# Start of a compressed interaction network: the order of the first chunk's tiles, and how fields and first weights are loaded

## What is computed

```
z = relu(sum over h, k of x0[b,h,d] * xk[b,k,d] * W[h,k,s] + bias[s])      s = 0..127
```

## Time and profile before

| | |
|---|---|
| median of 3 runs | 562.16 us |
| the profiled execution, its own time | 562.33 us |
| its span, first to last instruction | 560.5 us |
| PE busy | 551.9 us, 98% |
| DVE busy | 535.9 us, 96% |
| GpSimd (POOL) busy | 499.5 us, 89% |
| ACT busy | 379.4 us, 68% |
| DMA | 122.17 MB, mean 218 GB/s |

### The profile page before, as it was taken

One profiled execution on the slowest core, in us unless ns is written; L12 is line 12 of the kernel. 1 busy time (PEld: TensorE's weight loads), 2 busy tenths in 40 slices (PEclk: granted clock), 3 DMA queues, 4 the chain that ended last, 5 costly groups with the idle time before them and its releaser, 6 DMA issues.

```text
span 560.5 us, 6190 instructions
## 1 busy us (share of the span) xinstructions
PE 551.9 (98%) x2008; PEld 374.9 (67%) x2008; DVE 535.9 (96%) x496; ACT 379.4 (68%) x427; POOL 499.5 (89%) x228
## 2 busy tenths in 40 slices
PE   7999999999999999999999999999999999999997
PEld 2435667667677677777767677677777767677665
DVE  4679999999999999999999999999999999999985
ACT  0436577776858767676776858777676876858662
POOL 0438899899999989999899999989999899999986
PEclk9999999999999999999999999999999999999999
DMA  8997391844828266391845828276391845826200
GB/s 326 418 408 317 132 370 34 325 191 181 344 87 331 108 254 271 146 361 30 331 183 183 342 95 333 98 262 263 150 363 29 333 177 192 333 99 215 81 1 20
DMA packets 21056, 122.17 MB, mean 218 GB/s; under 512 B 2720, under 2 KB 2976, under 8 KB 10784
## 3 DMA queue, kind: packets, MB, share of 16 engines
q1 hardware_dynamic: 20736, 121.51, 56.0%
q10 hardware_dynamic: 288, 0.26, 0.2%
HBM read 121.24 MB, written 0.52 MB: 217 GB/s over the span
## 4 chain that ended last, share of the span: by engine, by line
PE 82%; DVE 10%; issue 3%; ACT 2%; DMA 1%; POOL 1%; SPq 0%; DVEq 0%; POOLq 0%; ACTq 0%
PE z L611 82%; DVE raw L426 4%; DVE exact L426 3%; DVE d_raw L426 2%; DMA fields<-x_fields 1%; DVE lo L440 1%; POOL lo L515 1%; ACT hi L656 1%; ACT maps L675 0%; ACT final L696 0%; ACT L675 0%; DVE sums L453 0%; DVE sums L447 0%; SPq L358 0%; SPq L337 0%
## 5 line engine op out<-in xcount | busy, mean ns | idle before, releaser
L515 POOL TENSOR_TENSOR lo<-raw,hi 128x1024 fp32r<-128x1024 f32 x198 | 469.1, 2410 | 12.1 <-ACT hi L656 11.6
L656 ACT ACTIVATE hi<-raw 128x1024 fp32r<-128x1024 f32 (+1 forms) x213 | 219.1, 1029 | 125.1 <-DVE raw L426 112.0
L611 PE MATMUL z<-hi,w_hi 128*128 128x512 f32 (+1 forms) x559 | 220.8, 399 | 0.9 <-ACT hi L656 0.4
L426 DVE TENSOR_TENSOR raw<-spread,maps 128x1024 f32<-128x1024 f32 x184 | 219.0, 1210 | 2.1 <-ACT maps L675 2.1
L611 PE MATMUL z<-hi,w_lo 128*128 128x512 f32 x513 | 202.5, 395 | 0.0
L611 PE MATMUL z<-lo,w_hi 128*128 128x512 f32 x544 | 196.7, 451 | 0.2 <-POOL lo L515 0.2
L611 PE MATMUL z<-exact,w_exact 128*128 128x512 f32 (+1 forms) x386 | 180.4, 594 | 2.8 <-DVE exact L426 2.0
L611 PEld LDWEIGHTS z<-lo,w_hi 128*128 128x128 f32 x544 | 101.2, 188 | 56.2 <-issue 31.5
L611 PEld LDWEIGHTS z<-hi,w_hi 128*128 128x128 f32 (+1 forms) x559 | 104.8, 188 | 31.4 <-ACT final L696 3.7
L611 PEld LDWEIGHTS z<-exact,w_exact 128*128 128x128 f32 (+1 forms) x386 | 72.1, 189 | 68.0 <-issue 53.7
L611 PEld LDWEIGHTS z<-hi,w_lo 128*128 128x128 f32 x513 | 96.2, 188 | 22.9 <-issue 0.5
(11 more groups left out here) (21 smaller groups left out, 69.6 us busy)
## 6 DMA issues: line engine op xcount, KB each, us to landing
spread<-x_spread SPq DMA_DIRECT2D x80, 1024.0 KB, 8.1
fields<-x_fields SPq DMA_DIRECT2D x31, 768.0 KB, 6.8
fields<-x_fields SPq DMA_DIRECT2D x15, 512.0 KB, 5.6
w_exact<-w SPq DMA_DIRECT2D x10, 256.0 KB, 14.7
spread<-x_fields SPq DMA_DIRECT2D x1, 768.0 KB, 10.1
raw<-w SPq DMA_DIRECT2D x1, 640.0 KB, 6.7
spread<-x_fields SPq DMA_DIRECT2D x1, 512.0 KB, 10.7
out<-sums SPq DMA_DIRECT2D x2, 240.0 KB, 4.2
```

Of the source, the lines that this page charges most:

```text
L426: nc.vector.tensor_tensor(products, by_field, by[0:rows, :].unsqueeze(1).to_broadcast([rows, tiles, COLS]), ALU.mult).then_inc(ready, 1)
L515: nc.gpsimd.tensor_tensor(low_part(layer, c, k), raw[low_rows(layer, k), PLACE[S][layer, c, k] % RAW_RING, 0:tiles_in(layer, k), :], hi[lo ...
L611: mm = nc.tensor.matmul(z_of(layer, c)[:, :], w[0:rows, :], part[0:rows, :], start=(step == FIRST_STEP[layer, c] and p == 0), stop=(step = ...
L656: nc.scalar.activation(hi[0:rows, count % HI_RING, 0:tiles, :], products, ACT.Copy).then_inc(hi_ready, 1)
```

## The change

- Layer 0 of chunk 0 runs its couples in the order 3, 0, 1, 2 (`FIRST_ORDER`), on DVE and on PE. Later chunks keep 0, 1, 2, 3.
- The tiles of layer 0 are stored one place further on: tile 6 stands in place 0, tiles 0 to 5 in places 1 to 6 (`place0`), in the fields and in w0. The inputs are rolled on the host to match.
- The fields of each chunk come in four loads of two slots (512 KB each) in place of three. The early fields come as slot 0 (256 KB) and twice two slots (512 KB each), in place of 768 and 512 KB. Of chunk 1's own fields, slots 0 and 1 and slots 6 and 7 are loaded (512 KB each), in place of slot 0 and slots 5 to 7.
- w0 comes in three parts of one, two and four tiles (128, 256, 512 KB), all issued by ACT ahead of the bias; before, two and five tiles (256 KB from ACT, 640 KB from SP). DVE adds them in three instructions.
- In chunks other than 1 DVE waits for load 0 and for the couple's own load ahead of each of the four couples: eight waits on fields a chunk in place of three.
- `W2_EARLY` is 0, so the two places where it stands change nothing.

```diff
-W0_CUTS = (0, 2, TILES0)
-W0_PARTS = 2
+FIRST_ORDER = (3, 0, 1, 2)
+W0_CUTS = (0, 1, 3, TILES0)
+W0_PARTS = 3
+W2_EARLY = 0
-FIELD_CUTS = (0, 3, 5, 1 + TILES0)
+FIELD_CUTS = (0, 2, 4, 6, 1 + TILES0)
+FIELD_PARTS = 4
...
-    yield 0, 0, range(COUPLES[0])
+    yield 0, 0, FIRST_ORDER
...
+        def place0(t):
+            return (t + 1) % TILES0
...
-            load_fields(0, 0)
-            sp.dma_start(w0_staged[:, W0_CUTS[1]:, :, :], w0[:, W0_CUTS[1]:, :, :]).then_inc(w0_loaded[1], 16)
-            load_fields(0, 1)
-            load_fields(0, 2)
+            for p in range(FIELD_PARTS):
+                load_fields(0, p)
             load_early(0)
             load_early(1)
...
+                        first = place0(2 * k)
+                        part = (k + 1) % FIELD_PARTS
                         if ahead:
-                            dve.wait_ge(early_loaded[k], 16)
-                        elif k < 3:
-                            dve.wait_ge(fields_loaded[k], (c if c and k == 1 else c + 1) * 16)
+                            dve.wait_ge(early_loaded[k], 16 if k else 32)
+                            by, by_field = early[:, 0, :], early[:, first:first + tiles, :]
+                        else:
+                            if c != 1:
+                                dve.wait_ge(fields_loaded[0], (c + 1) * 16)
+                            dve.wait_ge(fields_loaded[part], (c if c and part in (1, 2) else c + 1) * 16)
+                            by = copies if c else field_copies
+                            by_field = fields[0:rows, 1 + first:1 + first + tiles, :]
...
             for p in range(W0_PARTS):
                 sum_weights0(p)
-                multiply(0, 0, range(p, p + 1))
-            multiply(0, 0, range(W0_PARTS, COUPLES[0]))
+                multiply(0, 0, FIRST_ORDER[p:p + 1])
+            multiply(0, 0, FIRST_ORDER[W0_PARTS:])
...
-                        if (layer, c) == (0, 0) and k < W0_PARTS:
-                            pe.wait_ge(w0_summed, k + 1)
+                        if (layer, c) == (0, 0):
+                            pe.wait_ge(w0_summed, min(FIRST_ORDER.index(k) + 1, W0_PARTS))
...
-            act.dma_start(w0_staged[:, 0:W0_CUTS[1], :, :], w0[:, 0:W0_CUTS[1], :, :]).then_inc(w0_loaded[0], 16)
+            for p in range(W0_PARTS):
+                a, e = W0_CUTS[p:p + 2]
+                act.dma_start(w0_staged[:, a:e, :, :], w0[:, a:e, :, :]).then_inc(w0_loaded[p], 16)
```

More of the change, by code:

```diff
@@ L262, in cin_kernel @@
         early_loaded = [sem(f"early_loaded{p}") for p in range(EARLY)]
-        fields_loaded = [sem(f"fields_loaded{p}") for p in range(3)]
+        fields_loaded = [sem(f"fields_loaded{p}") for p in range(FIELD_PARTS)]
         spread_loaded = [sem(f"spread_loaded{s}") for s in range(SPREAD_RING)]
@@ L332, in load_fields @@
                 if c == 1:
-                    if p == 1:
+                    if p in (1, 2):
                         return
-                    e = 1 if p == 0 else e
                 sp.dma_start(fields[:, a:e, :], x_fields[c, :, a:e, :]).then_inc(fields_loaded[p], 16)
             def load_early(p):
-                a, e = FIELD_CUTS[p:p + 2]
-                sp.dma_start(early[:, a:e, :], x_fields[1, :, a:e, :]).then_inc(early_loaded[p], 16)
+                if p == 0:
+                    sp.dma_start(early[:, 0, :], x_fields[1, :, 0, :]).then_inc(early_loaded[0], 16)
+                sp.dma_start(early[:, 1 + 2 * p:3 + 2 * p, :],
+                             x_fields[1, :, 2 + 2 * p:4 + 2 * p, :]).then_inc(early_loaded[p], 16)
             def load_spread(c, q):
@@ L366, in _ @@
             load_fields(1, 0)
-            load_fields(1, 2)
+            load_fields(1, 3)
             for p in range(QUADS):
@@ L374, in _ @@
                     wait_multiplied(sp, 0, c + 1, COUPLES[0] - 1)
-                    for p in range(3):
+                    for p in range(FIELD_PARTS):
                         load_fields(c + 2, p)
@@ L400, in multiply @@
                         ahead = c == 1 and k < EARLY
+                        first = place0(2 * k)
+                        part = (k + 1) % FIELD_PARTS
                         if ahead:
-                            dve.wait_ge(early_loaded[k], 16)
-                        elif k < 3:
-                            dve.wait_ge(fields_loaded[k], (c if c and k == 1 else c + 1) * 16)
-                        by = early[:, 0, :] if ahead else copies if c else field_copies
-                        by_field = (early if ahead else fields)[0:rows, 1 + 2 * k:1 + 2 * k + tiles, :]
+                            dve.wait_ge(early_loaded[k], 16 if k else 32)
[6 more added lines that the diff above has]
+                            by_field = fields[0:rows, 1 + first:1 + first + tiles, :]
                     else:
@@ L468, in weights0_last_split_lo @@
                 rows, last = slice(2 * BLOCK, ROWS_REST), len(SPLIT_TILES[0]) - 1
-                nc.vector.tensor_tensor(w_hi[0][rows, last, :], w_exact[0][rows, TILES0 - 1, :],
+                nc.vector.tensor_tensor(w_hi[0][rows, last, :], w_exact[0][rows, place0(TILES0 - 1), :],
                                         w_hi[0][rows, last, :].bitcast(fp32),
@@ L537, in weights0_split_lo @@
                 pool.wait_ge(weights_hi[0], 1)
-                nc.gpsimd.tensor_tensor(w_lo[0][:, 0:tiles, :], w_exact[0][:, 0:tiles, :],
+                nc.gpsimd.tensor_tensor(w_lo[0][:, 0:tiles, :], w_exact[0][:, 1:1 + tiles, :],
                                         w_hi[0][:, 0:tiles, :].bitcast(fp32),
@@ L599, in contract @@
                                 rows = HALF
-                            passes += [(w_exact[layer][:, t, :],
+                            passes += [(w_exact[layer][:, t if layer else place0(t), :],
                                         exact[:, count % EXACT_RING, t % 2, :], rows)]
@@ L620, in _ @@
                 nc.tensor.matmul(z[2][:, :], final[:, 0:OUT], final[:, :], start=True, stop=True)
-            contract(0, 0, range(COUPLES[0]))
+            contract(0, 0, FIRST_ORDER)
             contract(0, 1, range(EARLY))
@@ L644, in split_hi @@
                 for k in couples:
-                    if c == 0 and (layer == 1 or layer == 2 and k < KEPT):
+                    if c == 0 and (layer == 1 or layer == 2 and W2_EARLY <= k < KEPT):
                         weights_split_hi(layer, 2 * k)
@@ L708, in _ @@
                     tiles = len(SPLIT_TILES[0]) - 1
-                    nc.scalar.activation(w_hi[0][:, 0:tiles, :], w_exact[0][:, 0:tiles, :], ACT.Copy)
-                    nc.scalar.activation(w_hi[0][0:ROWS_REST, tiles, :], w_exact[0][0:ROWS_REST, TILES0 - 1, :],
+                    nc.scalar.activation(w_hi[0][:, 0:tiles, :], w_exact[0][:, 1:1 + tiles, :], ACT.Copy)
+                    nc.scalar.activation(w_hi[0][0:ROWS_REST, tiles, :], w_exact[0][0:ROWS_REST, place0(TILES0 - 1), :],
                                          ACT.Copy).then_inc(weights_hi[0], 1)
@@ L722, in _ @@
                     split_hi(0, c + 1, range(0, MAPS2_AT) if c else range(EARLY, COUPLES[0]))
+                if c == 0:
+                    for k in range(W2_EARLY):
+                        weights_split_hi(2, 2 * k)
                 spread_maps2(c)
@@ L750 @@
     x_fields[:, :, 1:][:, used] = x[:, right[used]]
+    x_fields[:, :, 1:] = np.roll(x_fields[:, :, 1:], 1, axis=2)
     pair = np.concatenate([x, x[:, -1:]], axis=1).reshape(CHUNKS, TILES, 2, COLS)
@@ L759 @@
     pairs[both, 1] = w0[right[both], i[both]]
-    arrays = {"x_fields": x_fields, "x_spread": x_spread, "w0": pairs}
+    arrays = {"x_fields": x_fields, "x_spread": x_spread, "w0": np.roll(pairs, 1, axis=1)}
     for n, w in ((1, L0_rec_w1), (2, L0_rec_w2)):
```

## The result

The changed kernel takes 563.33 us (median of 10 runs, 563.18 to 564.23) where the kernel before takes 562.20 (10 runs, 562.08 to 562.73) on the same chip: 1.1 us slower, ratio 1.0021 with a 95% interval of 1.0011 to 1.0031. Nine of the ten stand at 563.18 to 563.49 with a mean granted clock of 0.997, one at 564.23 with 0.994. The forecast was 562.2 in a range of 561.4 to 562.9, so the time lies outside it, on the slower side. The profiled execution took 563.21 us with a span of 561.4; before, 562.33 and 560.5.

What follows compares the result with a forecast made beforehand. PE and DVE were taken as both full from 50 to 540 us, so start delays reach the end. Gain 1.06 and loss 1.10 left 0.04 us: 562.33 + 0.04 = 562.37, median 0.17 under, so 562.2; range 561.4 to 562.9.

Steps and rivals of the forecast that it cites:

- The frame: Start: its price is when layer 0 of chunk 0 is contracted and ACT's table load starts, 15.43 before, 15.47 forecast.
- Step 1: End of layer 0, chunk 0, on PE: tile 6 no longer runs last, gain 1.06 us.
- How loads share the engines: First loads: queues alternate by packet; landing is 3.81 us + 2.46 ns per KB ahead; rounds at 5.38, 7.27, 9.79, 11.05.
- Steps 2 and 3: Start: couple 0 on PE at 8.89, costing nothing; couple 1 at 11.68, 1.25 us later, awaiting w0's third part.
- Rival D: Start: PE falls to its lower clock while waiting before couples 0 and 1, costing 3.4 us, 565.6; chance 0.03.
- B: Start: w0's third part lands ahead of fields 2, at 8.53, 0.6 us won, 561.6; chance 0.20.
- C: Later chunks: DVE's 70 extra waits are not hidden, 0.016 to 0.05 us each, 563.3 to 565.7; chance 0.05.
- The cap: Layer 1's start: first `spread` load lands at 17.4, layer 1 starts at 18.08, limiting any gain to 0.7 us.

Runs made afterwards that it cites:

- experiment 1: Changed kernel with two more zero matmuls on PE between the twelve-row tile and couple 0: 562.86 us, ratio to the kernel before 1.0007.
- experiment 4: Changed kernel with its new loads and layout, but couples in the old order 0, 1, 2, 3 in the first chunk: 564.35 us, ratio 1.0034.
- experiment 5: Changed kernel with two more zero matmuls before couple 0 and first-chunk queues exchanged (ACT issues fields, SP w0 and bias): 562.55 us, ratio 1.0002.
- experiments 4 and 6: The second of these: changed kernel with five zero matmuls at the start in place of three: 562.86 us, ratio 1.0005.
- experiment 7: Changed kernel with three loads of fields, w0 in two parts (second from SP), bias on SP, five zero matmuls: 561.73 us, ratio 0.9988.
- experiment 11: Changed kernel with two more zero matmuls before couple 0, w0's third part from SP, bias on SP behind the early fields: 562.20 us, ratio 0.9993.
- experiment 2: Changed kernel with w0's third part issued by SP between its loads 1 and 2 of the fields: 563.40 us, ratio 1.0018.
- experiment 8: Kernel before with five more met DVE waits ahead of each layer 0 couple in chunks 2 to 15, 280 in all: 562.75 us, ratio 1.0003.
- experiment 9: Kernel before with two zero matmuls at the start in place of three: 563.48 us, ratio 1.0016.

## Why the prediction was wrong

- **The frame held.** The time of the table load was the one number to work out. At 16.52 it is outside the 14.8 to 15.9 that I had allowed it. It moved by 1.09 us; the end moved by 0.88 in the profiled executions (563.21 against 562.33) and by 1.13 in the medians. In the profiled pair 13 chunks took 436.36 us after and 436.56 before, 0.2 less; experiment 1, which has all of the change's waits and later loads, took 436.56 like the kernel before, so that difference is not the change's; what it is stays open.
- **Step 1 (tile 6 leaves the end, 1.06 us) was right in size:** the order alone moved the table load by 0.92 (experiment 4 against the changed kernel, both with the clock down), and couple 1 had started some 0.15 earlier in experiment 4 (12.08 against 12.23).
- **"How loads share the engines" failed in its sums for rounds 2 and 3 (a round is load n of SP with load n of ACT), and this is the first step that went wrong.** Alternation by packet was right, and SP's fields landed at 7.3 and 9.8 as forecast. But I read the landings of a kernel in which ACT's queue had one load ahead of its bias, and took the two loads of a round to land together. ACT's came at 5.6, 7.77 and 10.33, behind the fields by 0.2, 0.5 and 0.5 us. Experiment 5 showed the queue to be the reason for which of the two is late. That the whole round ends near 10.3 whichever queue is late is not explained by it: in the profiles of experiments 4 and 6, with the same loads, the fields came at 10.0 and 9.9, and w0's third part still at 10.3. The number of loads does not explain it either. The changed kernel issues three loads more ahead of `spread`, and the third of these lands at 24.09 instead of 23.68, 0.14 us a load; but experiment 7, with one load more than the kernel before, has it at 23.59, earlier and not later. Experiment 11 rules the bias out. Why the round is late stays open.
- **Steps 2 and 3 carried it on:** couple 0 on PE at 9.40, not 8.89, couple 1 at 12.23, not 11.68. With the clock up this is 0.49 us over the forecast (15.96 against 15.47, experiment 1). The time would then have been 562.9, the range's upper end, or by ratio (1.0007) 562.6, within it.
- **Rival D, at 0.03 and with no term in the sum, is what put the time outside: this is the second step that failed.** I had argued from one gap of 1.12 us in one profiled execution that such a gap does no harm, and forecast 1.1 us for the new one. It was 1.67, behind a twelve-row tile; and the kernel before seems to have been at the edge itself, with a clock of 0.997 in 23 of the 93 runs beside the experiments. Nor did the rows bear the argument out. The zero matmuls ahead of that gap were at 1.2 GHz to the last weight load (0.86 apart) and couple 0 behind it at 2.4: they show a clock that rose, not one that outlasted a gap. In the changed kernel's profile it was up ahead of the gap (the twelve-row tile's weight loads took 0.29 us, against 0.50 at the lower clock in experiment 11) and fell in it. D's price was wrong the other way: 3.4 us for two couples at half rate, where the low stretch covered couple 0 and the start of couple 1, much of it under the wait for w0, and 0.56 us was left.
- **Rivals B and C:** B's order of landing did not come by itself (w0's third part landed behind the fields of its round); made by hand it gave nothing with the clock down (experiment 2) and 0.66 with it up (562.86 to 562.20), close to the 0.6 of the rival. C is excluded by experiment 8.
- **The cap was not put to the test.** I had set it at 0.7 us by the first `spread` load, landed at 17.4. In experiment 7 that load landed at about 17.2 (issued at 5.28, 11.9 us to landing), layer 1 took it at 17.31, 0.77 us ahead of the kernel before, and all of this is there at chunk 14 (DVE's sums at 515.14 against 515.91).

## What to carry to other kernels

At a start that is bound by loads, work out how long TensorE is idle between its warm-up and its first real matmuls, over several runs and not in one profile: a gap that three runs in four bore at 1.1 us was borne by one of 22 at 1.7 (the changed kernel and experiment 2). A dummy matmul or two in the gap cost nothing in most profiles here and 0.2 us in one, where they ran past the moment at which the real operands were ready (experiment 11). Cutting the first loads finer let the first instruction start sooner here (5.67 against 6.38) and the last of them land later (`spread`, 24.09 against 23.68); cut only where something waits for the piece. Two late things in a row mask each other, so undo them together as well as one by one.

## What the hardware showed that was not expected

- What ACT's queue issued landed behind its partner on SP's in every round, by 0.2 to 0.5 us in the changed kernel and by 0.5 to 1.5 when the two were exchanged (experiment 5), though both issue their first load at 0.73 us.
- The loss to the lower clock varies from run to run of one kernel, in steps: 562.12, 563.4, 564.8 us with a mean clock of 1.000, 0.997, 0.994 (experiment 2). The one profile at 0.994 shows one low stretch from 8.7 to 15.5 us, where the changed kernel's at 0.997 has one from 9.3 to 12.7.
- The three zero matmuls that open each of these runs do not get the higher clock at the same time: in the profiles they end at 5.7 (experiment 1), 6.2 (experiment 2), 6.5 (the changed kernel) and 6.9 us (the kernel before).
- The record of the granted clock can say 1.00 at the start while the weight loads are 0.85 us apart (experiment 9), and so it does for the zero matmuls of the kernel before, which are 0.86 apart.
